# A fused cross-attention and FFN kernel: two sets of sums and per-tile order in the down projection

## What is computed

```python
x = x + xattn(layernorm(x), ctx)              # 8 x 1024 rows of 512, 16 heads, 64 context rows each
y = layernorm(x)
gate = fake_quant(y, clip_x) @ fake_quant_rows(w_gate).T        # 512 -> 1408
up   = fake_quant(y, clip_x) @ fake_quant_rows(w_up).T
h = fake_quant(silu(gate) * up, clip_down)    # scale = sigmoid(clip) * max|h| / 127 over ALL of h
x = x + h @ fake_quant_rows(w_down).T         # 1408 -> 512
# fake_quant(v) = clip(round(v / scale), -128, 127) * scale
```

## Time and profile before

| | |
|---|---|
| median of 3 runs | 1359.35 us (1358.99 to 1359.62) |
| the profiled execution | 1363.62 us |
| its span | 1361.9 us |
| TensorE clock granted, mean | 0.982 |
| PE busy | 1289.0 us (95%) |
| DVE busy | 1166.1 us (86%) |
| ACT busy | 787.2 us (58%) |
| POOL busy | 409.0 us (30%) |

### The profile page before, as it was taken

The page is one execution under the profiler, slowest core; times in us unless marked ns, Lnnn a source line. Parts: engine busy times, 40 slices in busy tenths (PEclk is TensorE's granted clock), DMA queues, the critical chain, the costliest instruction groups (busy, mean ns, idle before and its releaser), DMA issues.

```text
span 1361.9 us, 20412 instructions
## 1 busy us (share of the span) xinstructions
PE 1289.0 (95%) x7625; PEld 610.7 (45%) x7668; DVE 1166.1 (86%) x2059; ACT 787.2 (58%) x1183; POOL 409.0 (30%) x278
## 2 busy tenths in 40 slices
PE   7988999999999999999999999699999999799997
PEld 6433444544544445445444444344444444344343
DVE  6757899988988998889889857789999999789996
ACT  6557765776577557755764762233443443597671
POOL 2104424542454244424443521000000000045555
PEclk9998999999999999999999999899999999899999
DMA  7173525446246245362561335296666632299995
GB/s 286 43 220 105 128 81 158 135 124 202 74 127 216 64 148 163 109 205 59 155 219 54 115 125 131 101 284 218 204 253 254 252 104 63 93 391 423 424 400 189
DMA packets 179218, 241.72 MB, mean 177 GB/s; under 512 B 121632, under 2 KB 140848, under 8 KB 168112
## 3 DMA queue, kind: packets, MB, share of 16 engines
q1 hardware_dynamic: 179120, 240.43, 53.2%
HBM read 120.86 MB, written 90.57 MB: 155 GB/s over the span
## 4 chain that ended last, share of the span: by engine, by line
PE 71%; DVE 14%; ACT 5%; issue 4%; SPq 3%; DMA 2%; POOL 1%; POOLq 0%; DVEq 0%; ACTq 0%
PE pu L1482 10%; PE pg L1476 10%; PE pu L1510 7%; PE po L78 7%; PE po L80 7%; PE po L79 7%; PE ring L79 6%; PE ring L78 6%; PE ring L80 6%; DVE w L1448 2%; PE ring L1015 1%; ACT E L451 1%; DVE sg L1455 1%; PE ring L991 1%; SPq L1247 1%
## 5 line engine op out<-in xcount | busy, mean ns | idle before, releaser
L1351 ACT ACTIVATE sg<-pg,gate_scale 128x512 f32<-128x512 f32 x176 | 120.9, 687 | 186.9 <-PE pg L1476 186.9
L78 PE MATMUL ring<-yT,M 128*128 128x512 f16 x512 | 195.5, 382 | 0.0
L80 PE MATMUL ring<-yT,M 128*128 128x512 f16 x512 | 195.4, 382 | 0.0
L79 PE MATMUL ring<-yT,M 128*128 128x512 f16 x512 | 195.4, 382 | 0.0
L78 PE MATMUL po<-VW,p 128*128 128x512 f16 x480 | 182.8, 381 | 2.0 <-DVE p L633 2.0
L1476 PE MATMUL pg<-xqT,w 128*128 128x512 bf16 x689 | 179.5, 380 | 3.7 <-DMA xqT<-xq 2.0
L80 PE MATMUL po<-VW,p 128*128 128x512 f16 x480 | 182.7, 381 | 0.0
L79 PE MATMUL po<-VW,p 128*128 128x512 f16 x480 | 182.5, 380 | 0.0
L1482 PE MATMUL pu<-xqT,w 128*128 128x512 bf16 x690 | 179.7, 380 | 0.7
L1510 PE MATMUL pu<-w 128*128 128x512 bf16 x690 | 157.4, 386 | 19.6 <-DVE w L1450 10.1
L392 POOL TENSOR_TENSOR esum<-esum,E 128x512 f32<-128x512 f32 x96 | 131.0, 1365 | 76.3 <-ACT E L455 76.2
(11 more groups left out here) (239 smaller groups left out, 2152.4 us busy)
## 6 DMA issues: line engine op xcount, KB each, us to landing
hidden<-hb SPq DMA_DIRECT2D x11, 2816.0 KB, 9.7
hb<-hidden SPq DMA_DIRECT2D x11, 2816.0 KB, 18.4
xa<-x_rows_d SPq DMA_DIRECT2D x28, 1024.0 KB, 6.1
x<-in_x_dram SPq DMA_DIRECT2D x16, 1024.0 KB, 5.8
value_fold<-E SPq DMA_DIRECT2D x64, 256.0 KB, 2.5
VW<-value_fold SPq DMA_DIRECT2D x16, 1024.0 KB, 6.1
x_rows_d<-x SPq DMA_DIRECT2D x16, 1024.0 KB, 4.9
out_dram<-xa SPq DMA_DIRECT2D x12, 1024.0 KB, 12.7
```

The lines of the kernel that those rows point to most:

```text
L78: nc.tensor.matmul(out, a_hi, b_hi, start=first, stop=False)
L79: nc.tensor.matmul(out, a_hi, b_lo, start=False, stop=False)
L80: return nc.tensor.matmul(out, a_lo, b_hi, start=False, stop=last)
L1351: nc.scalar.activation(sg[:, n % 4], pg[n % 4][:], ACT.Silu, scale=gate_scale[:, n % FT:n % FT + 1]).then_inc(silus, 1)
```

## The change

- Two sets of four sums alternate: groups with even q add up in `pu`, with odd q in `pg`. Tile t waits for the taking of tile t two groups before.
- Group 0 is rounded in 11 parts of one block each, and its matmuls run block by block over the four tiles. The other groups are rounded in parts of 4, 4 and 3 blocks.
- On VectorE, both of groups 0 and 1 are rounded first, then the four tiles of group 0 are taken. From q = 1 on the order is: take tile 0, round part 0 of q + 1, take tile 1, round part 1, take tile 2, round part 2, take tile 3.
- In the last group the add of the last tile moves from GpSimd to VectorE, and the group is stored by tile (four stores of 256 KB for one of 1024 KB).
- A semaphore of the attention stage that nothing waits for (`c_hi`) is no longer made or raised, which makes room for `last_added`.

```diff
@@ -1224,7 +1224,7 @@
     r_loaded = [sem(f"r_loaded{k}") for k in range(4)]
     out_stored = [sem(f"out_stored{k}") for k in range(4)]
     down_scales, h_scaled, h_step, h_rounded = sem("down_scales"), sem("h_scaled"), sem("h_step"), sem("h_rounded")
-    downs, down_taken, added = sem("downs"), sem("down_taken"), sem("added")
+    downs, down_taken, added, last_added = sem("downs"), sem("down_taken"), sem("added"), sem("last_added")
     og = out.rearrange("b (j t p) d -> (b j) p t d", j=2, p=P)
     TURN_AT = 4
     HOME = [0, 1] * (NG // 2 - 3) + [0, 4, 2, 3, 0, 1]
@@ -1232,8 +1232,9 @@
     stores_of = lambda slot, g: sum(1 for k in range(min(g, KEPT)) if HOME[k] == slot)
     taken_as = lambda q: NG - 4 + q if q < 4 else q - 4
     h_slot = lambda q: 4 if q == NG - 1 else (2 + q) % 4
-    PARTS = ((0, 2), (2, 6), (6, FT))
-    NP = len(PARTS)
+    parts = lambda q: tuple((m, m + 1) for m in range(FT)) if q == 0 else ((0, 4), (4, 8), (8, FT))
+    parts_before = lambda q: sum(len(parts(k)) for k in range(q))
+    sums_of = lambda q: pu if q % 2 == 0 else pg
     def wait(eng, s, v):
         if v > 0:
             eng.wait_ge(s, v)
@@ -1291,7 +1292,7 @@
                 sp.dma_start_transpose(xqT[:, g % 2, :, t * P:(t + 1) * P], xq[:, t]).then_inc(x_turned[g % 2], 16)
 
         def load_h(q):
-            wait(sp, h_rounded, NP * (q - 3))
+            wait(sp, h_rounded, parts_before(q - 3) if q > 3 else 0)
             sp.dma_start(hb[:, h_slot(q)], h_d[taken_as(q)]).then_inc(h_loaded[h_slot(q)], 16)
 
         def load_r(q):
@@ -1319,12 +1320,21 @@
         for q in range(NG):
             if q + 5 < NG - 1:
                 load_h(q + 5)
-            sp.wait_ge(added, 4 * q + 4)
-            sp.dma_start(og[taken_as(q)], xa[(2 + q) % 4]).then_inc(out_stored[(2 + q) % 4], 16)
+            slot = (2 + q) % 4
+            if q < NG - 1:
+                sp.wait_ge(added, 4 * q + 4)
+                sp.dma_start(og[taken_as(q)], xa[slot]).then_inc(out_stored[slot], 16)
+            else:
+                for t in range(TT):
+                    if t < TT - 1:
+                        sp.wait_ge(added, 4 * q + t + 1)
+                    else:
+                        sp.wait_ge(last_added, 1)
+                    sp.dma_start(og[taken_as(q)][:, t], xa[slot][:, t]).then_inc(out_stored[slot], 16)
             if q + 3 < NG:
                 load_r(q + 3)
         for k in range(4):
-            sp.wait_ge(out_stored[k], 16 * NG // 4)
+            sp.wait_ge(out_stored[k], 16 * (NG // 4) + (16 * (TT - 1) if k == (2 + NG - 1) % 4 else 0))
 
     def on_gpsimd(pool):
         nc.gpsimd.memset(one[:, 9:10], 0.0).then_inc(magic_set, 1)
@@ -1340,7 +1350,7 @@
         for q in range(NG):
             slot = (2 + q) % 4
             pool.wait_ge(r_loaded[slot], 16 * (q // 4) + 16)
-            for t in range(TT):
+            for t in range(TT if q < NG - 1 else TT - 1):
                 pool.wait_ge(down_taken, 4 * q + t + 1)
                 nc.gpsimd.tensor_tensor(xa[slot][:, t], xa[slot][:, t], sg[:, t], ALU.add).then_inc(added, 1)
 
@@ -1440,26 +1450,35 @@
         dve.wait_ge(d_spread, 1)
         do_(nc.vector.tensor_scalar(down[:], pg[0][:], one[:, 6:7], None, ALU.mult))
 
-        def round_h(q):
-            slot = h_slot(q)
-            for n, (m0, m1) in enumerate(PARTS):
-                dve.wait_ge(h_scaled, FT * q + m1)
-                wait(dve, downs, 4 * (q - 1))
-                nc.vector.tensor_scalar(hq[:, q % 2, m0:m1], hb[:, slot, m0:m1], MAGIC, QMAX, ALU.subtract, ALU.min).then_inc(h_step, 1)
-                dve.wait_ge(h_step, NP * q + n + 1)
-                nc.vector.tensor_scalar(hq[:, q % 2, m0:m1], hq[:, q % 2, m0:m1], -QMAX - 1.0, None, ALU.max).then_inc(h_rounded, 1)
+        def round_h(q, n):
+
+            m0, m1 = parts(q)[n]
+            dve.wait_ge(h_scaled, FT * q + m1)
+            wait(dve, downs, 4 * (q - 1))
+            nc.vector.tensor_scalar(hq[:, q % 2, m0:m1], hb[:, h_slot(q), m0:m1], MAGIC, QMAX, ALU.subtract, ALU.min).then_inc(h_step, 1)
+            dve.wait_ge(h_step, parts_before(q) + n + 1)
+            nc.vector.tensor_scalar(hq[:, q % 2, m0:m1], hq[:, q % 2, m0:m1], -QMAX - 1.0, None, ALU.max).then_inc(h_rounded, 1)
 
         def scale_down(q, t):
             dve.wait_ge(downs, 4 * q + t + 1)
             wait(dve, added, 4 * (q - 1) + t + 1)
-            nc.vector.tensor_tensor(sg[:, t], pu[t][:], down[:], ALU.mult).then_inc(down_taken, 1)
-
-        round_h(0)
+            nc.vector.tensor_tensor(sg[:, t], sums_of(q)[t][:], down[:], ALU.mult).then_inc(down_taken, 1)
+
+        for n in range(FT):
+            round_h(0, n)
         for q in range(NG):
-            if q + 1 < NG:
-                round_h(q + 1)
+            more = q + 1 < NG
+            if q == 0:
+                for n in range(len(parts(1))):
+                    round_h(1, n)
             for t in range(TT):
                 scale_down(q, t)
+                if more and q > 0 and t < len(parts(q + 1)):
+                    round_h(q + 1, t)
+        q, slot = NG - 1, (2 + NG - 1) % 4
+        dve.wait_ge(down_taken, 4 * NG)
+        dve.wait_ge(r_loaded[slot], 16 * (q // 4) + 16)
+        nc.vector.tensor_tensor(xa[slot][:, TT - 1], xa[slot][:, TT - 1], sg[:, TT - 1], ALU.add).then_inc(last_added, 1)
 
     def on_tensor(pe):
         def up(g, i):
@@ -1498,16 +1517,24 @@
             ins = nc.tensor.matmul(pg[0][:, c * P:(c + 1) * P], ones[:], diag[:, c], start=True, stop=True)
         ins.then_inc(d_spread, 1)
         pe.wait_ge(w_turned[2], 16)
-        for q in range(NG):
+        def down_part(q, t, m):
+            return nc.tensor.matmul(sums_of(q)[t][:], hq[:, q % 2, m, t * P:(t + 1) * P], wd[:, m], start=(m == 0), stop=(m == FT - 1))
+
+        pe.wait_ge(hs, NG * FT)
+        for m in range(FT):
+            pe.wait_ge(h_rounded, m + 1)
             for t in range(TT):
-                wait(pe, down_taken, 4 * (q - 1) + t + 1)
-                if q == 0:
-                    pe.wait_ge(hs, NG * FT)
+                ins = down_part(0, t, m)
+                if m == FT - 1:
+                    ins.then_inc(downs, 1)
+        for q in range(1, NG):
+            for t in range(TT):
+                wait(pe, down_taken, 4 * (q - 2) + t + 1)
                 for m in range(FT):
-                    part = [n for n, (m0, m1) in enumerate(PARTS) if m0 == m]
+                    part = [n for n, (m0, m1) in enumerate(parts(q)) if m0 == m]
                     if t == 0 and part:
-                        pe.wait_ge(h_rounded, NP * q + part[0] + 1)
-                    ins = nc.tensor.matmul(pu[t][:], hq[:, q % 2, m, t * P:(t + 1) * P], wd[:, m], start=(m == 0), stop=(m == FT - 1))
+                        pe.wait_ge(h_rounded, parts_before(q) + part[0] + 1)
+                    ins = down_part(q, t, m)
                 ins.then_inc(downs, 1)
 
     return on_sync, on_gpsimd, on_scalar, on_vector, on_tensor
```

More of the change, by code:

```diff
@@ L167, in attention @@
     const_turned, step, sig = sem("const_turned"), sem("open_step"), sem("clip_exp")
-    c_centred, c_turned, c_hi, c_full, c_lo = sem("c_centred"), sem("c_turned"), sem("c_hi"), sem("c_full"), sem("c_lo")
+    c_centred, c_turned, c_full, c_lo = sem("c_centred"), sem("c_turned"), sem("c_full"), sem("c_lo")
     w_hi, w_lo = [sem("wk_hi"), sem("wv_hi")], [sem("wk_lo"), sem("wv_lo")]
@@ L518, in on_scalar @@
             act.wait_ge(c_turned, c + 1)
-            nc.scalar.activation(cT[:, 0, c, :], ring[c][:], ACT.Identity, scale=ccol[:, 0, c:c + 1], bias=ccol[:, 1, c:c + 1]).then_inc(c_hi, 1)
+            nc.scalar.activation(cT[:, 0, c, :], ring[c][:], ACT.Identity, scale=ccol[:, 0, c:c + 1], bias=ccol[:, 1, c:c + 1])
             nc.scalar.activation(cf[:, c], ring[c][:], ACT.Identity, scale=ccol[:, 0, c:c + 1], bias=ccol[:, 1, c:c + 1]).then_inc(c_full, 1)
```

## The result

The changed kernel takes 1368.72 us (median of 5 runs, 1368.07 to 1370.38) against 1359.35 for the kernel before; the ratio is 1.0062 with a 95% interval of 1.0051 to 1.0073, so 0.6% slower, 7 to 10 us. The forecast was 1366.8. The profiled execution took 1370.38 us and has a span of 1368.4 us.

A forecast was written before the change was run, and what follows sets the result against it. VectorE was taken to bound the kernel. Tile 0 of group 15 at 1200.35 + 0.7 + 14 x 11.19 = 1357.7, plus 7.8 and 3.8, gave span 1369.3 and median 1366.8 us, 0.55% slower; range 1358 to 1380.

The forecast's parts named there:

- The bound: Last stage, over one group: VectorE sets the pace at 10.42 us, not a shortage of banks.
- The group's cost: VectorE's new order: 3.76 + 3.42 + 3.02 + 0.99 = 11.19 us a group, against 10.42.
- The rule of exclusion by whole instructions: GpSimd's adds and VectorE's roundings run one instruction at a time; about 0.15 us of a rounding lies outside.
- Who gets the port: Rounding against GpSimd's add behind a taking: VectorE starts 0.2 us before the add and wins.
- add first: Rival, chance 0.18: GpSimd gets the port after tiles 1 and 2, 0.8 us more a group, 1378 us.
- The opening: Start of the stage: tile 0 of group 1 taken at 1200.35 instead of 1202.62, gain 2.3 us.
- The end: After the last taking: 3.8 us instead of 6.06, gain 2.3, at least 1.2; 256 KB lands in 2.5.
- the first round in the new order: First loop (q = 1): 0.7 us more, since group 0's four adds are still running.
- the clock only in group 0: TensorE's group 0: lower clock throughout would take back up to 3 us; nothing was counted.
- From the span to the median: Profiled execution 1371.0 us, less 4.3 by which the earlier profiled run exceeded its median: 1366.8.
- No more waiting than now: Rival, chance 0.12: waiting for adds stays 2.8 us, the group 10.42, the kernel 1356.0.
- TensorE could set the pace: Rival, chance 0.03: banks are the bound, 9.5 us a group until the last load, 1348 us.

The follow-up runs named there:

- the opening alone: Kernel before with only group 0 rounded in single blocks and its matmuls run block by block: 1361.62 us, ratio 0.9997.
- the kernel with the roundings together: Changed kernel with the next group's three roundings put together again ahead of the four takings: 1356.12 us, ratio 0.9971 to the kernel before.
- the end alone: Kernel before with only the last tile added by VectorE and the last group stored by tile: 1357.85 us, ratio 0.9980.
- the second profile: Changed kernel run again, nothing altered: 1367.74 us, ratio 1.0051 to the kernel before.

## Why the prediction was right

**The bound.** VectorE set the pace. Two sets of sums alone left the group at 10.42; taking GpSimd's adds out of the roundings' way brought 9.50, with one set of sums as with two.

**The group's cost.** 11.19 by the sum, 11.13 measured. By its pieces: tile 0 and its part 3.76 predicted, 3.70 measured (1268.33 to 1272.03); tile 1 3.42 and 3.42; tile 2 3.02 and 3.01; tile 3 0.99 and 1.00. The rule of exclusion by whole instructions, read off three rows of the kernel before, carried this.

**Who gets the port.** VectorE, at 0.15 or 0.16 us of lead, in all 27 such places of the profile; the rival "add first" did not occur. The two places in the earlier trace rows, won by GpSimd at 0.05 and by VectorE at about 0.24, bracketed it rightly; they stand with the same outcome in all 13 profiles.

**The opening.** I had tile 0 of group 1 taken 19.54 us after ScalarE's first scaling (1200.35 less 1180.81); it was 19.52 (1199.08 less 1179.56). But what I called a gain of 2.3 us is none by itself. The kernel before spent only 9.5 and 10.0 us in its next two rounds of VectorE's work, because group 0's first adds had run early, and the opening alone brought 0.1 us of stage. Only together with the parts of 4, 4 and 3 blocks and the two sets of sums does something remain: in the kernel with the roundings together tile 0 of group 1 is taken 27.56 us after the first scaling, 28.51 before. The sum was right since it went by absolute times; the name of the term was wrong.

**The end.** Predicted gain 2.3, measured 2.8 from the last taking on, and 2.8 in the stage of the end alone. The term was sized too small: 256 KB landed in 2.1 us, not in the 2.5 of the row I used.

**The term I missed.** For the first round in the new order I added 0.7 us, to 11.9; it took 12.67, and the next 12.05 for 11.19, 1.6 us more in all. 1.5 of it is TensorE's lower clock after it was starved, by the second profile, in which the clock held (12.04 and 11.14); and the adds of group 0 cost 0.9 and not 0.7. The prediction priced the clock only in group 0, and not where TensorE's lead over the rounding is used up. Against it stand twelve groups at 0.06 less than predicted, 0.7, and the end's 0.5. So the stage came out at 188.8 against a predicted 188.5 (1369.3 less 1180.8), with errors that cancelled. That the sum was so near is in part luck: in the second profile, without the fall of the clock, the stage took 187.3.

**From the span to the median.** The profiled execution came out at 1370.4 for 1371.0. I then took off 4.3 us, by which the profiled execution of the kernel before had lain above its median; after the change it was 1.7 (1370.38 less 1368.72). These 2.6 us of scatter between executions, less the 0.6, are why the median missed by 1.9 (1368.7 for 1366.8). The predicted 7.4 us lie in the interval of the ratio, 7 to 10 us, and in that of the repetition, 5 to 9 (1.0034 to 1.0067).

**The rivals.** "No more waiting than now" fell: spreading the adds raised the wait for them from 2.8 to 3.1 us a group, and 0.4 of waiting for TensorE came on top. That TensorE could set the pace is real, but it takes the adds out of the roundings' way, and then the transfers bind at 11.7 us a group.

## What to carry to other kernels

An engine that seems to wait for a free buffer may wait for the one that is to free it; look whether that one has idle time before buying more buffers. Where two engines exclude each other by whole instructions, count for each order which of them meet: here four takings in a row hid 1.6 us of adds, and spread out each taking hid less of one. Look also at what the last engine in the chain still has to do behind the last piece: one taking was too short to cover three matmuls. And moving work onto the busiest engine can pay, if it costs that engine less (0.6 us) than the wait it suffers when another does it (0.9 us).

## What the runs showed that I had not expected

TensorE's clock fell in mid-stage, after it had done 22 matmuls in one stretch of 5 us and 6 in the next. In another execution of the same kernel TensorE stood still at the same places and as long, and the clock held: 12.67 and 12.05 us for two groups in one, 12.04 and 11.14 in the other.

A change confined to the last stage went along with a later start of an early one: in both profiles of the kernel with all adds on VectorE the L78 products began some 3 us later than in the other eleven. Its last stage was 2.0 to 3.8 us shorter than the changed kernel's, and its timed runs were no faster. The cause is open, and so is whether the two belong together.
